# One ring of four PSUM banks for scans and dense stages, half stacks, and a new order of work in a two-layer attention kernel

## Chip, cores and metric

The kernel runs on one core of one Trainium2 chip. The metric is the device time of one execution in microseconds (us), the median of several runs; lower is better.

## What is computed

Two transformer blocks follow each other over `x` of 8 batches x 512 tokens x 256 features, all in float32. Both are modulated by a condition vector per batch. Each has 16 attention heads of 16 features. The first is causal and has a gelu MLP of width 1024; the second is not causal and has no MLP.

```python
# layer 0 (causal), cut
mod = silu(condition) @ Wada + bada          # shifts, scales, gates, one row a batch
xm = layernorm(x) * (1 + sc_a) + sh_a
q, k, v = split(xm @ Wqkv)                   # 16 heads of 16
attn = softmax(where(causal, q @ k.T * scale, -inf))
x = x + gt_a * ((attn @ v) @ Wproj + bproj)
xm = layernorm(x) * (1 + sc_m) + sh_m
x = x + gt_m * (gelu(xm @ W1 + b1) @ W2 + b2)
# layer 1, cut
h = gamma * layernorm(x) + beta
q, k, v = split(h @ Wqkv.T + bqkv)
h1 = (softmax(q @ k.T) / 16 @ v) @ Wp.T + bp + x
out = gamma * layernorm(h1) + beta + h1
```

## The kernel before

**Two passes over the scores.** The softmax needs each row's maximum, and the kernel gets it by computing the scores twice. A *scan* (token `s`) is one product of 128 query rows with the keys of one head, in bf16: `scan` on TensorE writes it into a PSUM bank `SX`, and VectorE reduces it to 128 maxima with one `reduce_max` (L738). Layer 0 scans are 128, 256, 384 and 512 columns wide, with a second small matmul for the causal mask (L936); layer 1 scans are 512 wide. A batch and layer has 64 scans, so the program has 1024. Later the same scores are computed again, transposed, in three banks `SC` (tokens `a` for three heads and `p` for the fourth), ScalarE takes their exponential into `E`, and the products with `V` (token `o`) accumulate in the bank `OP`, which ScalarE copies out (token `t`).

**Stacks.** To be exact enough in bf16, q and k are cut into three bf16 parts (`PART`), and 96 rows hold six products of parts. DMAs issued on SyncE (SP) bring the parts into these rows: six of 256 KB for a q stack (`stackq0`, `stackq1`) and six for a k stack (`stackk0`, `stackk1`). A scan waits on `stack_dma[layer]` for all twelve.

**Dense stages.** Everything else on TensorE goes through two banks `DN`: `turn_a`, `turn_m`, `turn_1` (transposes of the normed rows), `q0`, `k0`, `v0`, `q1`, `k1`, `v1`, `proj0`, `proj1`, `up_0` to `up_7`, `down_0` to `down_3`, and `max...` (transposes of the cut maxima, which POOL makes in `nm...`). ScalarE or VectorE reads each bank and adds to `dense_done`.

**Banks.** PSUM has eight: three `SC`, two `DN`, two `SX`, one `OP`. A dense stage waits for the dense reader two banks back, a scan for the scan reader two back. Neither ever waits for the other kind:

```python
wait(pe, dense_done, c.at(1, k - 1))          # bank(k), dense
return DN[(c.index() + k) % 2]
bank = SX[at["scan"].index() % 2]             # scan
wait(pe, scan_done, at["scan"].at(1, -1))
```

**Order.** All engines walk one list of tokens, written out by hand: `HEAD` (batches 0 and 1), `RING` once for each middle pass (five times), `TAIL` (the last ones). In a pass, layer 0 of batch i, layer 1 of batch i-1 and the first 41 scans of layer 0 of batch i+1 are woven together. Each engine executes its own instructions strictly in list order and waits on semaphores, so an instruction that waits holds back all that stands behind it on its engine. `pack`, `recip` and `scale` bring the softmax sums through DMAs to the projection: SP gathers sums and products (`RS`, `OC`), VectorE takes reciprocals (L873), SP writes and spreads them (`RB`), VectorE multiplies (L877). At the start, the modulation (`mods`, matmuls L888) stands between `q0` and `k0`, and `rows` (L978) behind.

Of the kernel before, what the change touches and what calls it, by code (L numbers as in the profile page):

```python
# [43 lines left out]
MASKED = -3.0e38  # L44

# [13 lines left out]
    stat_a norm_a turn_a q0 mods stackq0 k0 stackk0 rows s s s s s s s s s s s s s s s s s s nm0_0 s s max0_0 s  # L59
    s v0 s s s s s a row0 p s s s a s keep0 s p nm0_1 s s s s a s max0_1 s s s s p s s s s o s a s s s p a o s p  # L60
    a t nm0_2 s fold0_0 s s p a max0_2 p s o a p s s a s s p stat_a a o p s s s norm_a t a s fold0_1 p a s o s
    nm0_3 turn_a p max0_3 q0 a p o a p a t p o fold0_2 a p o t fold0_3 merge0 proj0 k0 stackq0 v0 norm_m turn_m
    stackk0 s s up_0 s s up_1 s s s s up_2 s s s s up_3 s s s s s s s s s up_4 s s up_5 s up_6 s s s s up_7 s s
    s s down_0 s s s s down_1 s s nm0a max0a down_2 s s down_3 s a s row0 s s norm_1 keep0 p a s s turn_1 s s s
    s q1 p s stackq1 stat_a o s k1 s stackk1 a v1 p a s s p a s s p o s s t a s s p s o s s s nm0b a s s p max0b
    s s s a s s s s s s p hold1 a p s o s a s s p s s s s s a s s s t p s s a s o s s s p a s s p o s nm1a s a s
    t s s p s s max1a s a s o p norm_a a s p a s p o s t s a p s pack0 s s recip0 a o turn_a p s s s q0 a scale0
    s v0 s p proj0 norm_m s a k0 o s t stackq0 p s a turn_m s s s up_0 s s up_1 stackk0 p s up_2 s up_3 s nm1b s
    s s a s up_4 s s up_5 s up_6 up_7 s p o s s max1b a s s down_0 s p s s a s s down_1 p s a o s s down_2 s s t
    p down_3 a o s s norm_1 p a s p s o t a s s s p s a s s nm0a p s o s a s p s turn_1 s s s max0a s a q1 p s  # L70
    k1""".split()
RING = """
    row0 o s s a stackq1 p s s a stackk1 t s p s s s s s s o s s a pack1 s s p s a row1 s p s s s a s s p s s nm0b
    s s recip1 o s s a s s p s s s max0b t s s s s a s scale1 p s a s o s s p a s o s p s a s p s t proj1 s a s p
    a o p a s p s s s o keep0 gain1 s t a s p s a o nm1a close1 s p s stat_a a max1a s v1 p s a o norm_a s t p s
    turn_a pack0 s a s s recip0 q0 s p s a o s stackq0 s p a scale0 s s p k0 a s s proj0 s s norm_m p v0 a o s p s
    t turn_m a s s o p s s a s up_0 s p stackk0 s up_1 s up_2 s s nm1b o s s up_3 s hold1 s up_4 s s max1b s s
    up_5 s s up_6 s s up_7 s s a s down_0 p s s a s down_1 s t p s down_2 s a s s p down_3 a o s p s a s p s s
    norm_1 o s s t a s s turn_1 s nm0a s s p s max0a a s o p s s a s q1 s p k1""".split()
TAIL = """  # L80
    s o row1 row0 a s t s s stackq1 stackk1 p s s a s p s s s s a s o s s s p s a p s s pack1 a s s o s p s s s
    nm0b a s s s p s t max0b s s a s o s s p s s a s p s recip1 a s s s o p s s a s s s s s p s a s t s s o p s
    s a s p s a s p s o nm1a s scale1 t a s s p max1a a o p s a p s proj1 a s p o gain1 s t v1 a s s pack0 p a s
# [37 lines left out]
for _n in ("norm_m", "norm_1", "norm_a"):  # L121
    ADDS[_n] = {"norm": 1}
ADDS["norm_m"]["bias"] = 1
COUNTS = ("dense", "res", "bias", "maxima", "max0", "max1", "hold", "pack", "sums", "scale", "rows0",
          "rows1", "x_in", "gain", "close", "stack0", "stack1", "high", "low", "norm", "head", "tick",
          "step", "masked", "group", "scan", "halves", "fold")


class Count:
# [999 lines left out]
```

## Time and profile before

| | |
|---|---|
| median of 3 runs | 1383.65 us (1379.31 to 1385.65) |
| the profiled execution | 1379.89 us, of which the span 1378.1 us |
| TensorE busy | 1242.5 us, 90% of the span |
| VectorE busy | 868.4 us, 63% |
| ScalarE busy | 672.3 us, 49% |
| GpSimd busy | 278.5 us, 20% |
| mean granted TensorE clock | 0.952 of 2.4 GHz |
| a middle pass | 151 to 154 us (the same product of the pass starts at 493.32, 647.43, 801.28 and 952.84 us) |

The span is the time from the first to the last instruction of the profiled execution. Busy time is the union of an engine's instructions. Matmuls overlap in the pipeline and their ends are modelled, so the busy time of TensorE also covers short waits between them; where two matmuls start is the surer measure. Names such as `SX<-KS,QS` say which tile is written from which; L933 is a line of the kernel.

### The profile page before, as it was taken

The numbers are of one execution on the slowest core, as the hardware profiler recorded it, in microseconds if no ns is written. First come the engines' busy times: TensorE is split into PE (matmuls) and PEld (weight loads), VectorE is DVE, ScalarE is ACT, GpSimd is POOL, SyncE is SP. The second block draws the span as 40 slices with busy tenths as digits, with TensorE's granted clock in tenths as the row PEclk, the third lists the DMA queues.
The fourth block names the chain that finished last, engine by engine and source line by source line (L and its number), as shares of the span: only waits on it lengthen the run. The fifth ranks groups of instructions, "written<-read, shape, count | busy, mean of one in ns | idle before, by whom it ended". The sixth has DMA issues, their size and how long they took to land.

```text
span 1378.1 us, 18596 instructions
## 1 busy us (share of the span) xinstructions
PE 1242.5 (90%) x6604; PEld 596.1 (43%) x6604; DVE 868.4 (63%) x1779; ACT 672.3 (49%) x1338; POOL 278.5 (20%) x378
## 2 busy tenths in 40 slices
PE   6687878999999998999899999999899998997786
PEld 4234443345344543446344543445344632453232
DVE  3553457654787467865787468865887477723664
ACT  1153224564555554655555565555456465555263
POOL 1123012120233012321132013311132012110002
PEclk9799988999999999999999999999999998999698
DMA  5603013130515024320515033510614050202101
GB/s 149 184 2 88 5 47 77 34 92 17 117 49 124 1 64 101 77 65 17 130 35 124 1 78 87 112 31 17 148 34 115 11 114 19 57 1 66 44 18 39
DMA packets 56118, 89.34 MB, mean 65 GB/s; under 512 B 9842, under 2 KB 20690, under 8 KB 56026
## 3 DMA queue, kind: packets, MB, share of 16 engines
q1 hardware_dynamic: 55006, 87.34, 26.4%
q8 instruction: 53, 0.87, 0.3%
q10 hardware_dynamic: 1020, 0.81, 0.2%
q14 instruction: 39, 0.32, 0.1%
HBM read 24.41 MB, written 4.70 MB: 21 GB/s over the span
## 4 chain that ended last, share of the span: by engine, by line
PE 69%; DVE 13%; ACT 6%; issue 2%; DMA 1%; POOL 1%; SPq 1%; ACTq 0%; DVEq 0%; POOLq 0%
PE DN L992 16%; PE OP L912 12%; PE SX L933 11%; PE SC L923 10%; DVE MX L738 9%; PE DN L1041 8%; PE DN L1017 7%; ACT E L599 4%; PE DN L1005 2%; PE SX L936 2%; DMA KS<-PART 1%; PE DN L1070 1%; DVE OUT L788 1%; SPq L476 1%; DVE PART L816 0%
## 5 line engine op out<-in xcount | busy, mean ns | idle before, releaser
L738 DVE TENSOR_REDUCE MX<-SX 128x1 f32<-128x512 f32 (+3 forms) x1024 | 556.4, 584 | 280.5 <-PE SX L936 174.0
L599 ACT ACTIVATE E<-SC 128x512 f32<-128x512 f32 (+3 forms) x1024 | 461.0, 523 | 383.6 <-PE SC L923 307.9
L933 PE MATMUL SX<-KS,QS 96*128 96x512 bf16 (+3 forms) x1024 | 342.7, 360 | 80.0 <-DVE MX L738 52.3
L923 PE MATMUL SC<-QS,KS 99*128 99x512 bf16 (+3 forms) x1024 | 280.8, 348 | 17.4 <-ACT E L599 10.1
L933 PEld LDWEIGHTS SX<-KS,QS 96*128 96x128 bf16 x1024 | 99.0, 98 | 294.7 <-DVE MX L738 172.9
L912 PE MATMUL OP<-E,V 128*32 128x512 f32 (+3 forms) x2048 | 216.5, 541 | 2.9 <-DVE X L808 1.4
L923 PEld LDWEIGHTS SC<-QS,KS 99*128 99x128 bf16 x1024 | 95.6, 99 | 164.8 <-ACT E L599 101.5
L517 POOL TENSOR_SCALAR_AFFINE_SELECT E<-E 128x512 f32<-128x512 f32 x128 | 85.7, 672 | 339.6 <-ACT E L599 339.6
L1041 PE MATMUL DN<-XT,W 128*128 128x512 f32 x256 | 123.7, 608 | 0.8 <-ACT HID L651 0.3
L1017 PE MATMUL DN<-XT,WQKV 128*128 128x512 f32 x256 | 121.8, 620 | 0.9 <-ACT XT L632 0.9
L992 PE MATMUL DN<-W,HID 128*128 128x256 f32 x512 | 117.1, 382 | 0.0
L936 PE MATMUL SX<-CAUSAL,ID 128*128 128x128 bf16 x512 | 112.6, 226 | 0.0
L912 PEld LDWEIGHTS OP<-E,V 128*32 128x32 f32 x2048 | 54.9, 112 | 110.1 <-issue 83.6
L992 PEld LDWEIGHTS DN<-W,HID 128*128 128x128 f32 x512 | 95.3, 190 | 14.1 <-ACT HID L651 0.3
L531 POOL TENSOR_TENSOR RSTD<-VE,HALF 128x4 f32<-128x4 f32 x32 | 32.9, 1029 | 296.1 <-DVE VE L750 295.3
L651 ACT ACTIVATE HID<-DN,VF 128x512 f32<-128x512 f32 x64 | 44.0, 687 | 66.7 <-PE DN L1041 66.2
L1017 PEld LDWEIGHTS DN<-XT,WQKV 128*128 128x128 f32 x256 | 49.1, 199 | 53.5 <-issue 49.1
L844 DVE TENSOR_TENSOR TMP<-DN,ROW 128x512 f32<-128x512 f32 x32 | 22.0, 689 | 78.2 <-PE DN L992 78.2
L552 POOL TENSOR_SCALAR NMP<-MX 128x32 bf16<-128x32 f32 (+1 forms) x36 | 8.6, 240 | 279.7 <-DVE MX L738 232.6
L992 PE MATMUL DN<-WP,OC 128*128 128x256 f32 x256 | 63.6, 406 | 1.4 <-ACT OC L657 1.4
L1041 PEld LDWEIGHTS DN<-XT,W 128*128 128x128 f32 x256 | 45.8, 192 | 42.7 <-issue 33.5
L936 PEld LDWEIGHTS SX<-CAUSAL,ID 128*128 128x128 bf16 x512 | 51.5, 101 | 25.6 <-issue 14.7
(92 smaller groups left out, 915.5 us busy)
## 6 DMA issues: line engine op xcount, KB each, us to landing
QS<-PART SPq DMA_DIRECT2D x96, 256.0 KB, 4.8
KS<-PART SPq DMA_DIRECT2D x96, 256.0 KB, 6.5
OC<-OE SPq DMA_DIRECT2D x56, 128.0 KB, 5.4
RB<-recip_sums SPq DMA_DIRECT2D x56, 128.0 KB, 2.6
XIN<-in_x SPq DMA_DIRECT2D x8, 512.0 KB, 4.2
ROW<-row_vectors SPq DMA_DIRECT2D x8, 512.0 KB, 3.6
out<-OUT SPq DMA_DIRECT2D x7, 512.0 KB, 3.2
W<-in_w SPq DMA_DIRECT2D x2, 1024.0 KB, 8.2
```

Source lines behind the costliest of these rows:

```text
L517: g.affine_select(out=block, in_=block, compare_op=ALU.is_ge, fill=zero, base=0, pattern=[[0, 4], [1, P]], channel_multiplier=-1)\
L531: g.tensor_tensor(RSTD[:], VE[:], HALF[:], ALU.pow).then_inc(rstd_pool, 1)
L599: a.activation(E[:, at["tick"].index() % 3, j, lo:T], SC[(at["head"].index() + j) % 3][:, lo:T], ACT.Exp, scale=HD ** -0.5 if layer == 0 e ...
L651: a.activation(HID[:, ht, :], bank(0)[:], ACT.Gelu, bias=B1[:, ht:ht + 1])\
L738: v.reduce_max(MX[:, qt, h:h + 1], SX[at["scan"].index() % 2][:, 0:w], AX.X, negate=True)\
L912: ins = t_.matmul(OP[32 * j:32 * j + 32, lo:T], V[layer][:, kt, h * VW:h * VW + 32], E[:, (at["step"].index() + n) % 3, j, lo:T], start=kt ...
L923: t_.matmul(SC[(at["head"].index() + j) % 3][:, lo:T], KS[layer][0:ALL_ROWS, h, kt * P:kt * P + P], QS[layer][0:ALL_ROWS, h, lo:T], start= ...
L933: ins = t_.matmul(bank[:, 0:w], QS[layer][0:CUT_ROWS, h, qt * P:qt * P + P], KS[layer][0:CUT_ROWS, h, 0:w], start=True, stop=layer == 1)
L936: ins = t_.matmul(bank[:, qt * P:w], ID16[:], CAUSAL[:], start=False, stop=True)
L992: ins = t_.matmul(psum[:, t % 2 * D:t % 2 * D + D], rows[:, kt, t * P:t * P + P], weights(kt), start=kt == 0, stop=kt == depth - 1)
L1017: ins = t_.matmul(psum[:], WQKV[n][:, kt, lo:lo + P], XT[:, kt, :], start=kt == 0, stop=kt == KT - 1)
L1041: ins = t_.matmul(psum[:], W1[:, kt, ht * P:ht * P + P], XT[:, kt, :], start=kt == 0, stop=kt == KT - 1)
```

## The change

Four things change. First, the banks `DN` and `SX` become one ring of four, `X`. Each scan takes one turn in it, and each dense stage one or two; a pair of `down` stages shares one. The new function `claim` lets TensorE wait for the last reader of the bank that it takes, whichever kind that reader was. Second, a stack is loaded in two halves of eight heads: twelve DMAs of 128 KB instead of six of 256 KB, with a semaphore for each half, so that scans of heads 0 to 7 wait for the first half only; the columns of the q and k weights are reordered on the host so that a half is 64 partitions. Third, at the start `k0` stands ahead of `mods`. Fourth, all three lists are new.

```diff
+BANKS = 4
...
-    stat_a norm_a turn_a q0 mods stackq0 k0 stackk0 rows s s s s s s s s s s s s s s s s s s nm0_0 s s max0_0 s
...
+    stat_a norm_a turn_a q0 stackq0 k0 mods stackk0 rows s s s s v0 s s s s s s s s s s s s s s s s s nm0_0 s s
...
+for _n, _adds in ADDS.items():
+    if "dense" in _adds and not _n.startswith("down"):
+        _adds["bank"] = _adds["dense"]
+ADDS["down_0"]["bank"] = ADDS["down_2"]["bank"] = 1
...
-        DN = [pb(f"DN{i}", [P, T]) for i in range(2)]
-        SX = [pb(f"SX{i}", [P, T]) for i in range(2)]
+        X = [pb(f"X{i}", [P, T]) for i in range(BANKS)]
...
-                    for part, ready in enumerate(marks[what[5:]]):
-                        wait(sp, (high_act, cut_low, cut_low)[part], ready)
-                        for r in range(CUTS):
-                            if parts[r] == part:
-                                sp.dma_start((QS, KS)[side][n][r:CUT_ROWS:CUTS, :, :], PART[:, side, part, :, :])\
-                                    .then_inc(stack_dma[n], 16)
+                    for half in range(2):
+                        rows = slice(P // 2 * half, P // 2 * half + P // 2)
+                        heads = slice(H // 2 * half, H // 2 * half + H // 2)
+                        for part, ready in enumerate(marks[what[5:]]):
+                            wait(sp, (high_act, cut_low, cut_low)[part], ready)
+                            for r in range(CUTS):
+                                if parts[r] == part:
+                                    sp.dma_start((QS, KS)[side][n][r:CUT_ROWS:CUTS, heads, :],
+                                                 PART[rows, side, part, :, :]).then_inc(stack_dma[n][half], 16)
...
+            def claim(n, done, value):
+
+                if n - BANKS in last_read:
+                    before, count = last_read.pop(n - BANKS)
+                    wait(pe, before, count)
+                last_read[n] = (done, value)
...
-                    wait(pe, stack_dma[layer], 192 * (b + 1))
-                bank = SX[at["scan"].index() % 2]
-                wait(pe, scan_done, at["scan"].at(1, -1))
+                    wait(pe, stack_dma[layer][h // (H // 2)], 192 * (b + 1))
+                claim(at["bank"].at(), scan_done, at["scan"].at(1, 1))
+                bank = X[at["bank"].index() % BANKS]
...
-                    wait(pe, dense_done, c.at(1, k - 1))
-                    return DN[(c.index() + k) % 2]
+                    if what in ("down_1", "down_3"):
+                        return X[marks["down"]]
+                    claim(at["bank"].at(1, k), dense_done, c.at(1, k + 1))
+                    marks["down"] = (at["bank"].index() + k) % BANKS
+                    return X[marks["down"]]
...
-        return w.reshape(-1, H // 2, 2, HD).transpose(0, 2, 3, 1).reshape(-1, D)
+        return w.reshape(-1, 2, H // 4, 2, HD).transpose(0, 3, 1, 4, 2).reshape(-1, D)
```

The first place is TensorE at the very start. L1017 (now L1044) is a projection of q or k, L888 (L903) the modulation, L978 (L1002) the gate rows, L933 (L957) a scan. Before:

```order
L1017 MATMUL DN0<-XT,WQKV0 128x512 x2
L1017 MATMUL DN1<-XT,WQKV0 128x512 x2
L888 MATMUL SC1<-CS,HID 128x8 x16
L888 MATMUL SC1<-CT,E 128x8 x8
L1017 MATMUL DN0<-XT,WQKV0 128x512 x2
L1017 MATMUL DN1<-XT,WQKV0 128x512 x2
```

and with the change:

```order
L1044 MATMUL X2<-XT,WQKV0 128x512 x2
L1044 MATMUL X3<-XT,WQKV0 128x512 x2
L1044 MATMUL X0<-XT,WQKV0 128x512 x2
L1044 MATMUL X1<-XT,WQKV0 128x512 x2
L903 MATMUL SC1<-CS,HID 128x8 x16
L903 MATMUL SC1<-CT,E 128x8 x8
```

The four matmuls of K now follow those of Q, and the modulation comes behind them.

The second place is TensorE in a middle pass, some 10 us behind `k1`, where scans of layer 0 stand densest. L912 (L927) is the product with V, L923 (L938) a score. Before, six scans stand in a row:

```order
L933 MATMUL SX0<-KS0,QS0 128x384
L936 MATMUL SX0<-CAUSAL,ID16 128x128
L933 MATMUL SX1<-KS0,QS0 128x512
L936 MATMUL SX1<-CAUSAL,ID16 128x128
L933 MATMUL SX0<-KS0,QS0 128x128
L936 MATMUL SX0<-CAUSAL,ID16 128x128
L933 MATMUL SX1<-KS0,QS0 128x256
L936 MATMUL SX1<-CAUSAL,ID16 128x128
L933 MATMUL SX0<-KS0,QS0 128x384
L936 MATMUL SX0<-CAUSAL,ID16 128x128
L933 MATMUL SX1<-KS0,QS0 128x512
L936 MATMUL SX1<-CAUSAL,ID16 128x128
```

and with the change, at the same place of the pass:

```order
L957 MATMUL X0<-KS0,QS0 128x512
L960 MATMUL X0<-CAUSAL,ID16 128x128
L957 MATMUL X1<-KS0,QS0 128x128
L960 MATMUL X1<-CAUSAL,ID16 128x128
L927 MATMUL OP<-E,V0 32x512 x4
L927 MATMUL OP<-E,V0 32x384 x4
L957 MATMUL X2<-KS0,QS0 128x256
L960 MATMUL X2<-CAUSAL,ID16 128x128
L957 MATMUL X3<-KS0,QS0 128x384
L960 MATMUL X3<-CAUSAL,ID16 128x128
L957 MATMUL X0<-KS0,QS0 128x512
L960 MATMUL X0<-CAUSAL,ID16 128x128
```

The product now stands among the scans instead of behind six of them, and the banks go round in fours. The longest run of scans in `RING` is four instead of six, and the count of scans that are third or later in their run is 14 instead of 9.

The third place is TensorE in `TAIL`, where layer 1 of the last batch begins. Before, the scans come right behind the last product of the batch ahead:

```order
L1017 MATMUL DN1<-XT,WQKV1 128x512 x2
L912 MATMUL OP<-E,V1 32x512 x8
L933 MATMUL SX0<-KS1,QS1 128x512
L933 MATMUL SX1<-KS1,QS1 128x512
L933 MATMUL SX0<-KS1,QS1 128x512
```

and with the change `v1` (L1019) comes first:

```order
L1044 MATMUL X3<-XT,WQKV1 128x512 x2
L927 MATMUL OP<-E,V1 32x512 x8
L1019 MATMUL X0<-WQKV1,XT 128x256 x4
L1019 MATMUL X1<-WQKV1,XT 128x256 x4
L957 MATMUL X2<-KS1,QS1 128x512
L957 MATMUL X3<-KS1,QS1 128x512
L957 MATMUL X0<-KS1,QS1 128x512
```

The matmuls of `v1` moved ahead of the first scan that needs the K stack.

## Rows read from the trace of the kernel before

**Rows 1.** The page: the chain that ended last, by engine.

```profile
PE 69%; DVE 13%; ACT 6%; issue 2%; DMA 1%; POOL 1%; SPq 1%; ACTq 0%; DVEq 0%; POOLq 0%
```

**Rows 2.** Waits of TensorE, whole span: us in total, times, longest us.

```profile
PE SX L933 <- DVE MX L738: 52.3, 174, 2.9
PE SX L933 <- DMA KS<-PART: 22.2, 3, 11.8
```

**Rows 3.** Stretches of a middle pass: PE, PEld, DVE, ACT, POOL busy, clock, DMA.

```profile
665.00:675.00 10.00, 8.68 (x59) 2.79 (x62) 8.53 (x16) 4.88 (x10) 1.28 (x2) 1.00 1.06 228
675.00:685.00 10.00, 8.86 (x69) 3.57 (x61) 8.45 (x18) 4.75 (x14) 2.80 (x7) 1.00 0.60 143
685.00:695.00 10.00, 8.91 (x39) 2.85 (x39) 8.92 (x14) 4.12 (x13) 2.29 (x2) 0.71 0.38 111
...
705.00:715.00 10.00, 8.59 (x67) 2.90 (x70) 9.62 (x24) 6.58 (x18) 6.36 (x9) 1.00 0.00 0
715.00:725.00 10.00, 9.86 (x74) 6.16 (x67) 9.49 (x28) 5.21 (x13) 2.71 (x5) 1.00 0.18 58
```

**Rows 4.** Timeline of that pass, VectorE and TensorE: start us, us, what.

```profile
683.59 0.54 DVE L873 RECIPROCAL RR<-RS 128x64 f32<-128x64 f32 x1
684.07 6.89 DVE L738 TENSOR_REDUCE MX<-SX 128x1 f32<-128x512 f32 x11
...
743.76 3.62 PE L992 MATMUL DN<-WQKV,XT 128*128 128x256 f32 x16
```

**Rows 5.** Timeline of the start, TensorE, VectorE and SP.

```profile
16.62 5.40 PE L1017 MATMUL DN<-XT,WQKV 128*128 128x512 f32 x8 [0.92 <-ACT XT L632]
...
22.68 3.88 SPq L476 DMA_DIRECT2D QS<-PART  x6
...
24.14 1.23 DVE L816 TENSOR_TENSOR PART<-X,PART 128x1024 bf16<-128x1024 f32 x1
...
27.33 5.17 PE L1017 MATMUL DN<-XT,WQKV 128*128 128x512 f32 x8
...
42.63 0.29 PE L933 MATMUL SX<-KS,QS 96*128 96x128 bf16 x1 [8.82 <-DMA KS<-PART]
```

**Rows 6.** Timeline of VectorE in the first scans.

```profile
45.90 0.98 DVE L738 TENSOR_REDUCE MX<-SX 128x1 f32<-128x256 f32 x2 [0.40 <-PE SX L936]
47.13 0.89 DVE L738 TENSOR_REDUCE MX<-SX 128x1 f32<-128x512 f32 x2 [0.25 <-PE SX L936]
48.42 0.98 DVE L738 TENSOR_REDUCE MX<-SX 128x1 f32<-128x256 f32 x2 [0.40 <-PE SX L936]
```

**Rows 7.** DMA issues of the page: KB each, median us to landing.

```profile
OC<-OE SPq DMA_DIRECT2D x56, 128.0 KB, 5.4
RB<-recip_sums SPq DMA_DIRECT2D x56, 128.0 KB, 2.6
```

**Rows 8.** Timeline of TensorE where batch 1's K stack is awaited.

```profile
139.36 0.23 PE L933 MATMUL SX<-KS,QS 96*128 96x128 bf16 x1 [1.65 <-DMA KS<-PART]
```

**Rows 9.** Waits of TensorE for scan reductions, window 140:330 us.

```profile
PE SX L933 <- DVE MX L738: 12.7, 33, 2.9
```

**Rows 10.** Waits of TensorE for scan reductions, window 1104:1240 us.

```profile
PE SX L933 <- DVE MX L738: 6.1, 19, 0.9
```

**Rows 11.** Timeline of the last batch's layer 1, TensorE and SP.

```profile
1266.05 1.92 PE L912 MATMUL OP<-E,V 128*32 128x512 f32 x16
1279.72 1.03 PE L933 MATMUL SX<-KS,QS 96*128 96x512 bf16 x2 [11.75 <-DMA KS<-PART]
...
1282.58 1.21 PE L933 MATMUL SX<-KS,QS 96*128 96x512 bf16 x2 [0.19 <-DVE MX L738]
```

**Rows 12.** SP in the same stretch.

```profile
1263.73 4.07 SPq L476 DMA_DIRECT2D QS<-PART  x6
1267.85 4.25 SPq L476 DMA_DIRECT2D KS<-PART  x6
```

**Rows 13.** SP behind `stackk1` in the middle pass.

```profile
671.98 0.59 SPq L414 DMA_DIRECT2D RS<-OE  x1
```

More of the change, by code:

```diff
@@ L64 @@
[L64 to L68, printed above, removed]
@@ new lines @@
+    turn_1 s a s s stat_a s q1 s p a s k1 stackq1 p s s o v1 s t a s s p s s s s s stackk1 s a s s nm0b p s
+    max0b s a o s p s a s o norm_a s s p s a p s t s s a s o p s s a p s a s s p s s s o s a t s s p turn_a s o
+    s a s p s a s p s s nm1a s o s t q0 max1a s pack0 recip0 v0 stackq0 s s s a s hold1 s s p s a p s o scale0 s
+    a proj0 p k0 a s p s norm_m s a s s o s s p turn_m stackk0 t s a s up_0 up_1 s p up_2 s s up_3 s up_4 up_5 s
+    s s s a s s up_6 s nm1b up_7 s s s p s o s s a s max1b p s down_0 down_1 s s a s o s p s down_2 s s a s p
@@ L234, in one_list @@
             at["scan"].n += 1
+            at["bank"].n += 1
         else:
@@ L356, in two_layers @@
         max_dma = [sem("max_dma0"), sem("max_dma1")]
-        stack_dma = [sem("stack_dma0"), sem("stack_dma1")]
+        stack_dma = [[sem(f"stack_dma{n}{half}") for half in "ab"] for n in range(2)]
         sums_dma = sem("sums_dma")
@@ L624, in bank @@
                     wait(act, dense_full, c.at(1, k + 1))
-                    return DN[(c.index() + k) % 2]
+                    return X[(at["bank"].index() + k) % BANKS]
                 if what in ("turn_a", "turn_m", "turn_1"):
@@ L637, in work @@
                     side = "qk".index(what[0])
-                    wait(act, stack_dma[0], at["stack0"].at(192))
-                    wait(act, stack_dma[1], at["stack1"].at(192))
+                    for half in range(2):
+                        wait(act, stack_dma[0][half], at["stack0"].at(192))
+                        wait(act, stack_dma[1][half], at["stack1"].at(192))
                     for t in range(2):
@@ L765, in bank @@
                     wait(dve, dense_full, c.at(1, k + 1))
-                    return DN[(c.index() + k) % 2]
-                if what == "mods" and b == 0:
+                    if what in ("down_1", "down_3"):
+                        return X[marks["down"]]
+                    return X[(at["bank"].index() + k) % BANKS]
+                if what in ("down_0", "down_2"):
+                    marks["down"] = at["bank"].index() % BANKS
+                elif what == "mods" and b == 0:
                     modulation()
```

57 lines of the change are left out of this document (30 added, 27 removed).

## The prediction

> **What bounds the kernel now.** I read the chain that ended last first. TensorE holds 69% of it and VectorE 13% [rows 1], so TensorE's own work sets most of the time, and what can be won is where it stands still. Next I read the waits of TensorE over the whole span. One wait leads, scan matmuls waiting for the reduction of an earlier scan, 52.3 us in 174 waits; three waits for K stacks add 22.2 us [rows 2]. Both are what the change is about, so 74.5 us is visible to it. More is hidden, because a short wait between two pipelined matmuls still reads as busy.
>
> The next question is whether a deeper ring can win these waits back or whether VectorE is itself full there. For this I read one middle pass in stretches of 10 us. In 665 to 695 and 705 to 725 TensorE has its holes, and VectorE is busy 8.53, 8.45, 8.92, 9.62 and 9.49 us of 10 [rows 3]. So in the 50 us where scans stand densest VectorE works for 45.0 us and idles 5.0. The timeline agrees: eleven reductions of 512 columns run for 6.89 us without a hole, 0.63 us each, while TensorE waits for them [rows 4]. More banks do nothing for such a burst except to let TensorE run two scans further ahead. This is the main reason why I don't forecast all of the 52.3 us.
>
> **The start.** Today Q's matmuls end at 16.62 + 5.40 = 22.0 us, the modulation follows, K's start at 27.33, and the first scan starts at 42.63 after 8.82 us of waiting for the K stack [rows 5]. With K directly behind Q, its matmuls run from 22.0 to about 26, or to 27.2 at the 5.17 us that they took. From Q's last matmul to the end of its last cut VectorE needed 24.14 + 1.23 - 22.0 = 3.4 us [rows 5]; K needs the same, so its parts are ready at 29.4 to 30.6. SP then is the limit: the Q stack has twelve issues now. An issue takes 3.88/6 = 0.65 us at 256 KB [rows 5]. For 128 KB I take the same 0.65, since `OC` and `RB` of 128 KB are issued at nearly that pace. Twelve from 22.68 end at 30.4, the six of K's first half at 34.3, and the last lands 2.6 us after its issue by the 128 KB rows of `RB` [rows 7]: first scan at about 36.3 instead of 42.6. TensorE is free by then: the modulation, which filled 22.0 to 27.3, ends near 32. Gain **6.3 us**; bounds 3 (the landing takes 5.4 as for `OC`, [rows 7]) and 9 (half an issue's price for half the bytes).
>
> **The first scans.** From the start only scans run, and TensorE and VectorE wait for each other through two banks: four tiles take 48.42 - 45.90 = 2.52 us, of which VectorE reduces 0.98 + 0.89 = 1.87 [rows 6]. With four banks VectorE should run through: 0.47 us a tile instead of 0.63, over the 27 tiles that stand ahead of the first score **4.3 us**; bounds 0 and 4.3. Seventeen further scans move into this time, ahead of the first score.
>
> **Batch 1's K stack.** Two scans stood ahead of `up_0` and waited 1.65 us [rows 8]; now `up_0` and `up_1` come first. **1.7 us**, bounds 0 and 1.7.
>
> **140 to 330 us.** TensorE shows 12.7 us of waits for reductions, the longest 2.9 [rows 9]. Some are of the short kind that four banks remove, some are bursts; I take half, **6 us**, bounds 0 and 12.7.
>
> **The five middle passes.** The 5.0 us of VectorE idle above are one part of what can be won. The other is borrowing: TensorE may enter a dense stage or a product with two more scans queued for VectorE, 2 x 0.63 us in each of the two stretches, 2.5 us. Together 7.5 us is the upper bound, nothing the lower. I take **4.4 us** a pass, somewhat over half, because products hold no bank and dense stages hold two of the four: ahead of products the queue really doubles, ahead of dense stages it doesn't. Also the densest burst of six is broken up while the lists as a whole put no fewer scans third in a run. Five passes: **22 us**, bounds 0 and 37.
>
> **The end.** The last batch's layer 1 has nothing else to do while its stacks load: TensorE stands from about 1268 to 1279.72 [rows 11]. `v1` fills 3.5 us of it (a `v` stage takes 3.62 us, [rows 4]). The K half: SP issues twelve DMAs from 1263.73 to 1272.10 today [rows 12], 3 MB that land by 1279.7. The change issues eighteen up to the end of K's first half, to about 1263.7 + 18 x 0.65 = 1275.4, and the last lands 2 to 2.6 us later: 1277.6, only **2.1 us** sooner, since Q's second half now goes ahead of K's first. Together **5.6 us**, bounds 3 and 7. The Trainium skill (DMA: Bandwidth & Descriptors, Rules for kernel authors) advises against splitting a transfer over partition halves, since both halves use the same DMA engines one after the other. The stacks here bear that out in bytes (3 MB in about 16 us either way), and by that rule alone the 2.1 us would be nothing, but a reader that needs only one half can gain from it. Behind it, pairs of scans of layer 1 take 1.21 + 0.19 = 1.40 us at half clock [rows 11], 0.70 a tile against 0.63 for VectorE alone [rows 4]: 18 tiles, **1.3 us**. The last passes, 1104 to 1240 us, show 6.1 us of waits [rows 10]; half is **3 us**.
>
> **What is added.** `claim` itself is a semaphore wait in place of another. SP issues 24 more DMAs a pass, 15.6 us; where that could be felt is the second rival. I cost them at nothing.
>
> **Sum.** 6.3 + 4.3 + 1.7 + 6 + 22 + 5.6 + 1.3 + 3 = 50.2 us. The profiled execution took 1379.9, so 1329.7; it lies 3.8 us under the median of the runs, which makes **1333**. All terms at their lower bounds leave 6 us of gain (1378), all at the upper ones 80 (1304).
>
> **Rivals.**
> *The middle passes don't move (1364).* If VectorE is the limit of the dense stretches [rows 3, 4], TensorE arrives earlier and waits longer, and only start, first scans, batch 1's stack and end are won: 6.3 + 4.3 + 1.7 + 5.6 + 1.3 = 19.2 us, 1383.7 - 19.2 = 1364. For it: 96% in 705 to 715. Against it: 85% in the two stretches before. 17%.
> *SP late for the sums (1343).* `pack1` stands behind `stackk1` on SP, and VectorE stands still at the reciprocal until `RS` has landed, with every scan behind it. Today `RS` is issued at 671.98 [rows 13] and the reciprocal runs at 683.59 without a wait [rows 4]: 11.6 us, less 5.4 to land [rows 7] leaves 6.2. Twelve more issues are 7.8 us. So 1.6 us are missing in each of six passes, about 10 us. Against it: in the new list Q is projected earlier before K, and SP can start sooner. It shrinks the gain and doesn't turn it. 10%, mostly inside my range.
> *Slower (1405).* Dense stages and scans now wait for each other. A pass has 36 dense claims, the program 288. In a ring of four a dense stage behind a burst finds a bank whose reduction is still queued on VectorE, and then waits up to one reduction, 0.63 us; all matmuls, scores too, stand behind it. At 0.25 us each it costs 72 us against 50 gained: 1405. It decides from 0.18 us a claim. For it: VectorE is up to 96% busy [rows 3], and today no such wait can exist. Against it: at such a place the next scan would have met the same backlog, so most of it takes the place of a wait that is there today. 8%.
> *The clock (1348).* 685 to 695 has a granted clock of 0.71 [rows 3]: TensorE fell from 2.4 to 1.2 GHz after 20 us with holes, for 5.8 us, which costs at most half of that, 2.9. If holes come in another rhythm and one such stretch more falls in each of five passes, 15 us are lost: 1348. The Trainium skill (TensorE: Matmul & The Clock Gate, A second HAM failure mode) tells of a kernel that went round PSUM banks and lost clock by small idle times between groups; the ring has that form, but here holes exist before and shrink. 5%.
> *The change wins no time (within 0.5%, 1377 to 1390)*: 6%. *More than I count, under 1315*, since hidden waits are won too: 8%.
>
> **Numbers.** The forecast case, 1315 to 1350, has 46% alone and takes in the SP case; with the clock and deeper cases around it the range 1304 to 1365 leaves out about 2 in 10. Its low end is all upper bounds, its high end the case in which the middle passes don't move. A measurement of this kernel tells 0.5% (7 us) from no change. Faster by more than that: 86%; within it: 6%; slower: 8%.
>
> **What would show it.** First scan near 36 us; reductions of the first scans back to back; a middle pass some 4 us shorter; waits of scans for reductions well under 52.3 us in total, with VectorE above 90% in the dense stretches; the gap before the last layer 1's scans near 6 us. I am wrong if the reciprocal (L873's successor) waits for `RS`, if dense lines show waits for reductions of scans, or if the passes keep their length.

## The result and the profile after

The changed kernel takes **1286.9 us** (median of 4, 1285.2 to 1290.0) against 1381.5 for the kernel before on the same chip: the ratio is **0.932** [0.929, 0.935]. That is faster, as forecast, but by 94.6 us where 50 were forecast, and below the low end of the range (1304). The profiled execution took 1288.15 us, its span is 1286.4.

The page of the changed kernel: the engines' busy time, the granted clock in 40 slices (tenths), the chain that ended last by engine, and the issues of the stacks.

```profile
PE 1198.2 (93%) x6604; PEld 593.7 (46%) x6604; DVE 858.4 (67%) x1779; ACT 688.6 (54%) x1356; POOL 273.5 (21%) x378
...
PEclk9789999999999999999999999999999999999698
...
PE 69%; ACT 9%; SPq 8%; DVE 7%; issue 3%; DMA 3%; POOL 1%; ACTq 0%; DVEq 0%; POOLq 0%
...
QS<-PART SPq DMA_DIRECT2D x192, 128.0 KB, 2.3
KS<-PART SPq DMA_DIRECT2D x192, 128.0 KB, 2.4
```

VectorE fell from 13% to 7% of the chain [rows 1]; ScalarE and SP's issues took over part of it. The mean granted clock of the span rose from 0.952 to 0.969.

TensorE's waits in the changed kernel over the whole span (us in total, times, longest us). L957 is the scan (L933 before), L938 a score, L1019, L1032, L1068 and L1097 are dense stages.

```profile
PE SC L938 <- ACT E L607: 12.0, 39, 1.2
PE X L957 <- DMA KS<-PART: 8.9, 3, 5.5
PE X L957 <- DVE MX L747: 8.9, 35, 0.8
PE X L1032 <- DVE XN L797: 5.9, 2, 4.5
...
PE X L957 <- ACT HID L660: 1.9, 7, 0.7
```

The 52.3 us of [rows 2] are 8.9, and the 22.2 us for K stacks are 8.9 too. These two rows account for 56.7 of the 91.7 us between the two spans. The rest has no row of its own: it lies in waits too short to show as one, and in the clock. To see it I added up, for every matmul, the time from its start to the start of the next, less what its columns take at 2.4 GHz. Of this excess the lower clock gets its share of the time by the granted clock at that time, and the rest is standing still, put down to what the next matmul was.

| us, whole span | before | changed | ring_only | order_only | order_ring | scan_two | scan_three |
|---|---|---|---|---|---|---|---|
| still ahead of scans | 137.5 | 47.9 | 84.3 | 204.0 | 58.0 | 218.6 | 99.0 |
| still ahead of scores | 54.2 | 63.0 | 65.6 | 53.1 | 63.9 | 50.6 | 56.6 |
| still ahead of dense stages | 39.3 | 46.2 | 53.6 | 40.4 | 46.5 | 33.6 | 40.0 |
| all standing still | 243.4 | 173.8 | 217.5 | 299.1 | 182.6 | 299.4 | 205.6 |
| lower clock | 55.8 | 34.6 | 52.1 | 103.3 | 29.2 | 117.5 | 44.8 |

(The last five are kernels of the experiments below. "All" holds products with V and masks too.) From the first matmul to the last, what is left when both are taken off is 1063 to 1070 us in every kernel. From before to changed, standing still falls by 69.6 us and the clock's cost by 21.2, 90.8 together, nearly the 91.7 between the spans. Ahead of scans alone TensorE won 89.6 us, and 20 came back elsewhere, 15.7 of them ahead of scores and dense stages. The split between the last two rows is a choice, since time that TensorE stands still at the lower clock could go to either. If the clock is charged only with the second time that columns take at 1.2 GHz, its cost is 46 us before and 28 changed, and standing still falls by 74 us: the two parts are good to some 4 us.

By stages, counted from the start of each `up_0`, against the terms of the prediction:

| stretch | before, us | changed, us | won | forecast |
|---|---|---|---|---|
| start to first `up_0` | 139.7 | 125.9 | 13.8 | 12.3 |
| to the second `up_0` | 150.9 | 131.3 | 19.6 | 6 |
| next five passes, each | 157.9, 154.1, 153.9, 151.5, 151.7 | 151.5, 145.4, 147.4, 144.6, 145.8 | 6.4, 8.7, 6.5, 6.9, 5.9 | 4.4 |
| to the last `up_0` | 150.3 | 143.8 | 6.5 | 3 |
| from it to the end | 168.1 | 150.7 | 17.4 | 6.9 |

The last two lines of the table belong together. The new `TAIL` takes 21 matmuls, some 6 us of TensorE's own work, ahead of the last `up_0` instead of behind it (587 matmuls behind it before, 566 changed), so 6 of the 17.4 us were moved and not won there. Together the two stretches won 23.9 us where the terms make 9.9. The last stretch before and then changed, in the columns explained below:

```profile
1209.99:1378.14 168.15, 134.90 (x587) 57.18 (x587) 78.43 (x149) 74.48 (x132) 18.50 (x28) 0.88 0.14 34
```

```profile
1135.68:1286.40 150.72, 126.97 (x566) 54.44 (x566) 74.31 (x144) 68.98 (x126) 16.54 (x27) 0.90 0.14 38
```

The windows of two other stretches show both effects. Columns: window, us; busy time and count of PE, PEld, DVE, ACT, POOL; granted clock; DMA share; GB/s. In the kernel before:

```profile
139.70:290.60 150.90, 132.98 (x645) 64.03 (x643) 95.82 (x192) 57.50 (x119) 29.12 (x38) 0.90 0.23 52
602.60:756.50 153.90, 147.79 (x810) 71.45 (x810) 106.84 (x219) 83.26 (x168) 34.83 (x44) 0.98 0.29 69
```

and in the changed kernel:

```profile
125.90:257.20 131.30, 121.53 (x641) 61.69 (x641) 91.66 (x185) 54.90 (x116) 29.52 (x38) 0.96 0.23 67
554.10:701.50 147.40, 143.48 (x810) 71.62 (x810) 104.76 (x219) 87.48 (x171) 34.22 (x45) 0.99 0.26 72
```

Busy TensorE time itself fell, by 11.5 us in the first stretch with nearly the same matmuls (641 for 645): a matmul at 1.2 GHz reads as a longer busy one. In the middle pass the 810 matmuls are the same, and VectorE's 219 instructions too, yet the pass is 6.5 us shorter. VectorE was busy 106.8 of 153.9 us there, so over the whole pass it wasn't full, only over the dense stretch.

The start and the end, where single steps can be read. The changed kernel's SP and TensorE at the start (start us, us, engine, line, what):

```profile
22.76 8.28 SPq L484 DMA_DIRECT2D QS<-PART  x12
31.09 7.65 SPq L484 DMA_DIRECT2D KS<-PART  x12
...
36.64 0.29 PE L957 MATMUL X<-KS,QS 96*128 96x128 bf16 x1 [1.35 <-DMA KS<-PART]
...
45.41 0.39 PE L957 MATMUL X<-KS,QS 96*128 96x512 bf16 x1 [0.20 <-DVE MX L747]
...
47.00 0.39 PE L957 MATMUL X<-KS,QS 96*128 96x512 bf16 x1 [0.20 <-DVE MX L747]
```

The first scan starts at 36.64 (forecast 36.3, before 42.63 [rows 5]). Four tiles take 47.00 - 45.41 = 1.59 us, against 2.52 before [rows 6], and VectorE reduces 22 tiles in a row without a hole:

```profile
43.67 8.57 DVE L747 TENSOR_REDUCE MX<-X 128x1 f32<-128x128 f32 x22
```

And its end, TensorE and SP:

```profile
1189.26 1.92 PE L927 MATMUL OP<-E,V 128*32 128x512 f32 x16
1191.11 3.72 PE L1019 MATMUL X<-WQKV,XT 128*128 128x256 f32 x16
1200.29 10.44 PE L957 MATMUL X<-KS,QS 96*128 96x512 bf16 x19 [5.46 <-DMA KS<-PART]
```

The gap ahead of the last layer 1's scans is 5.46 us where it was 11.75 [rows 11]; near 6 was forecast. In SP's queue the time from `QS`'s first issue to the first scan is 1200.29 - 1186.95 = 13.3 us, where it was 1279.72 - 1263.73 = 16.0 [rows 11, 12].

```profile
1186.95 7.70 SPq L484 DMA_DIRECT2D QS<-PART  x12
1194.69 7.66 SPq L484 DMA_DIRECT2D KS<-PART  x12
```

### The profile page after: what moved, and what is told of

The parts are those of the page before. It is cut to its first block, busy times and chain, and to the rows that moved or that the text cites. A ratio compares the mean times of both kernels' runs of the same rounds, so it can differ in the third digit from the quotient of the medians.

```text
span 1286.4 us, 18823 instructions
## 1 busy us (share of the span) xinstructions
PE 1198.2 (93%) x6604; PEld 593.7 (46%) x6604; DVE 858.4 (67%) x1779; ACT 688.6 (54%) x1356; POOL 273.5 (21%) x378
## 4 chain that ended last, share of the span: by engine, by line
PE 69%; ACT 9%; SPq 8%; DVE 7%; issue 3%; DMA 3%; POOL 1%; ACTq 0%; DVEq 0%; POOLq 0%
PE X L1019 17%; PE OP L927 12%; PE SC L938 10%; PE X L957 10%; PE X L1068 8%; PE X L1044 8%; ACT E L607 7%; SPq L484 6%; DVE MX L747 3%; PE X L1032 2%; DMA OC<-OE 2%; PE X L960 1%; SPq L421 1%; PE X L1097 1%; DVE XN L797 1%
## 5 line engine op out<-in xcount | busy, mean ns | idle before, releaser
L747 DVE TENSOR_REDUCE MX<-X 128x1 f32<-128x512 f32 (+3 forms) x1024 | 535.9, 585 | 182.2 <-PE X L960 111.7
L957 PE MATMUL X<-KS,QS 96*128 96x512 bf16 (+3 forms) x1024 | 309.4, 353 | 22.6 <-DMA KS<-PART 8.9
L938 PE MATMUL SC<-QS,KS 99*128 99x512 bf16 (+3 forms) x1024 | 284.0, 347 | 21.7 <-ACT E L607 12.0
L927 PE MATMUL OP<-E,V 128*32 128x512 f32 (+3 forms) x2048 | 212.9, 533 | 4.2 <-ACT OE L622 3.1
L938 PEld LDWEIGHTS SC<-QS,KS 99*128 99x128 bf16 x1024 | 95.4, 98 | 192.0 <-ACT E L607 116.8
L957 PEld LDWEIGHTS X<-KS,QS 96*128 96x128 bf16 x1024 | 98.6, 99 | 175.3 <-DVE MX L747 59.8
L1068 PE MATMUL X<-XT,W 128*128 128x512 f32 x256 | 121.9, 607 | 3.3 <-ACT XT L640 2.7
L1044 PE MATMUL X<-XT,WQKV 128*128 128x512 f32 x256 | 118.2, 605 | 1.0 <-ACT XT L640 1.0
L1019 PE MATMUL X<-W,HID 128*128 128x256 f32 x512 | 115.6, 381 | 0.5 <-ACT HID L660 0.5
L960 PE MATMUL X<-CAUSAL,ID 128*128 128x128 bf16 x512 | 106.3, 223 | 0.0
L927 PEld LDWEIGHTS OP<-E,V 128*32 128x32 f32 x2048 | 54.5, 111 | 107.7 <-issue 73.8
L1019 PEld LDWEIGHTS X<-W,HID 128*128 128x128 f32 x512 | 96.0, 190 | 15.3 <-issue 1.1
L1044 PEld LDWEIGHTS X<-XT,WQKV 128*128 128x128 f32 x256 | 47.5, 194 | 52.3 <-issue 47.7
L1068 PEld LDWEIGHTS X<-XT,W 128*128 128x128 f32 x256 | 46.3, 192 | 47.6 <-issue 44.6
L1019 PE MATMUL X<-WP,OC 128*128 128x256 f32 x256 | 60.4, 389 | 2.4 <-issue 0.8
L960 PEld LDWEIGHTS X<-CAUSAL,ID 128*128 128x128 bf16 x512 | 51.3, 100 | 23.9 <-issue 11.0
```

The source lines that it names most:

```text
L747: v.reduce_max(MX[:, qt, h:h + 1], X[at["bank"].index() % BANKS][:, 0:w], AX.X, negate=True)\
L927: ins = t_.matmul(OP[32 * j:32 * j + 32, lo:T], V[layer][:, kt, h * VW:h * VW + 32], E[:, (at["step"].index() + n) % 3, j, lo:T], start=kt ...
L938: t_.matmul(SC[(at["head"].index() + j) % 3][:, lo:T], KS[layer][0:ALL_ROWS, h, kt * P:kt * P + P], QS[layer][0:ALL_ROWS, h, lo:T], start= ...
L957: ins = t_.matmul(bank[:, 0:w], QS[layer][0:CUT_ROWS, h, qt * P:qt * P + P], KS[layer][0:CUT_ROWS, h, 0:w], start=True, stop=layer == 1)
L960: ins = t_.matmul(bank[:, qt * P:w], ID16[:], CAUSAL[:], start=False, stop=True)
L1019: ins = t_.matmul(psum[:, t % 2 * D:t % 2 * D + D], rows[:, kt, t * P:t * P + P], weights(kt), start=kt == 0, stop=kt == depth - 1)
```

## The experiments

The experiments ran at three later times, on three chips, where the kernel before took 1381.4 us (the parts apart), 1381.5 (depth and half reductions) and 1383.8 (the single steps). The ratios are to the kernel before on the same chip at the same time. Where kernels of different times are compared and differ by 2 to 6 us, the medians alone don't settle it.

Two theories stood first for the 44 us that the forecast missed. **A, depth**: four banks let TensorE run ahead, and that wins more than I allowed. **B, order**: the new lists space scans better, and win on their own. Later came **D**, the new lists live on scans that run three or four deep, and its rival **E**, what the new lists need of the ring is banks for the dense stages.

### The parts apart

**ring_only**: the kernel before with the ring of four and its claims; old lists and whole stacks. A pair of `down` stages keeps its bank of the ring while the scans between them go round, so three scans of `HEAD` that stood between `down_0` and `down_1` stand ahead of `down_0`.

```diff
-        DN = [pb(f"DN{i}", [P, T]) for i in range(2)]
-        SX = [pb(f"SX{i}", [P, T]) for i in range(2)]
+        X = [pb(f"X{i}", [P, T]) for i in range(BANKS)]
...
-                wait(pe, scan_done, at["scan"].at(1, -1))
+                claim(at["bank"].at(), scan_done, at["scan"].at(1, 1))
```

> The lists and the whole stacks of before, with the ring of four banks (three scans of batches 0 and 1 are moved from behind down_0 to ahead of it, since a pair of down stages holds a bank). Theory A (depth: short waits for a scan bank, visible and hidden, are what is won, and any order wins them): 1325 to 1345, waits of scans for reductions under 20 us. Theory B (order: the lists move VectorE's load out of the dense stretches, the ring alone only lets TensorE arrive earlier at the same VectorE): 1360 to 1378, waits of scans still over 35 us.

Measured: 1350.4 us, 0.975 [0.972, 0.978]; 31 us won. That lies between the two forecasts; the waits (12.9 us, below) are those of theory A.

**order_only**: the changed kernel with its new lists, but two banks for scans, two for dense stages and whole stacks.

```diff
-        X = [pb(f"X{i}", [P, T]) for i in range(BANKS)]
+        DN = [pb(f"DN{i}", [P, T]) for i in range(2)]
+        SX = [pb(f"SX{i}", [P, T]) for i in range(2)]
...
-                claim(at["bank"].at(), scan_done, at["scan"].at(1, 1))
+                wait(pe, scan_done, at["scan"].at(1, -1))
```

> The new lists (K behind Q with them) with two dense and two scan banks and whole stacks. Theory A (depth): only start and end are won, 1355 to 1375, and scans wait for reductions 45 us or more. Theory B (order): most is won, 1305 to 1330.

Measured: 1489.1 us, 1.075 [1.071, 1.080]; **108 us slower** than before, which neither theory had.

**order_ring**: the changed kernel with whole stacks, so new lists and ring.

```diff
-                    wait(pe, stack_dma[layer][h // (H // 2)], 192 * (b + 1))
+                    wait(pe, stack_dma[layer], 192 * (b + 1))
```

> New lists and ring, whole stacks. If half stacks are worth what the start and the end show (first scan and last layer-1 scan some 2 to 4 us sooner each): 1290 to 1296. If the twelve shorter issues also matter in the middle passes through the sums behind them on SP, it would be faster than the change: under 1285.

Measured: 1292.9 us, 0.935 [0.931, 0.938].

**order_half**: new lists and half stacks, with two and two banks as in order_only.

> New lists and half stacks, two dense and two scan banks. Against the full change this takes the ring alone away. Theory A (depth): 1345 to 1370. Theory B (order): 1297 to 1320.

Measured: 1477.0 us, 1.067 [1.064, 1.070], again far outside both.

The first three and the kernel before make a square:

| us | old lists | new lists |
|---|---|---|
| two and two banks | 1381 | 1489 |
| ring of four | 1350 | 1293 |

The ring is worth 31 us under the old lists and 196 under the new ones; the new lists cost 108 us without the ring and win 57 with it. Both theories fall: the gain is in neither part, and a sum over the parts, which my prediction was, can't give it. Half stacks win 12 us without the ring (1489.1 to 1477.0, same chip and time) and perhaps 6 in it (1292.9 to 1286.9, at two times and with intervals that overlap).

TensorE's waits show the same. In order_only:

```profile
PE SX L933 <- DVE MX L738: 122.8, 261, 3.0
PE SC L923 <- ACT E L599: 12.5, 40, 1.2
PE SX L933 <- DMA KS<-PART: 12.5, 3, 8.6
```

and in ring_only:

```profile
PE X L953 <- DMA KS<-PART: 22.8, 4, 11.8
PE X L953 <- DVE MX L743: 12.9, 57, 0.5
PE SC L934 <- ACT E L604: 12.6, 45, 0.6
PE X L953 <- ACT HID L656: 11.6, 18, 1.5
```

The last row there is new. Under the old lists the ring ends the waits for reductions (52.3 to 12.9, none over 0.5 us), and 11.6 us return as scans that wait for ScalarE to read an `up` stage's bank: the shared ring's own wait, the reverse of the one that my slower rival named. The new lists have 1.9 of it. By the count in the result's table the ring wins 53.2 us ahead of scans under the old lists, and 25.7 of them return ahead of scores and dense stages: TensorE runs ahead with its scans and then stands at the next thing. Under the new lists the ring wins 146.0 ahead of scans, and 16.9 return (order_only against order_ring). A middle pass (the same columns as above), first of ring_only, then of order_only:

```profile
583.80:736.70 152.90, 145.73 (x810) 71.86 (x809) 106.75 (x219) 82.77 (x167) 33.74 (x44) 0.98 0.30 69
```

```profile
638.40:809.00 170.60, 153.34 (x810) 72.41 (x810) 107.77 (x219) 88.19 (x171) 34.11 (x44) 0.95 0.28 62
```

With the old lists the ring wins 1 us in this pass (152.9 for 153.9), with both 6.5 are won, and new lists alone lose 17. Over all five middle passes, from the second `up_0` to the seventh, the ring alone wins 0.2 us in all, both together 34.4 (6.9 a pass), and the new lists alone lose 77.7 (15.5 a pass). What the ring wins under the old lists lies wholly outside the middle passes: 6.1 us up to the first `up_0`, 10.0 up to the second, 7.3 up to the last and 5.9 behind it.

What do the new lists ask for? On TensorE, where tokens of other engines don't break a run of scans, 17 scans of a middle pass stand third or later in their run instead of 12 (not the 14 and 9 given with the change). Here is how long TensorE stood still ahead of scans in the same pass, by their place in the run. The clock is charged as in the second split above and the floor is the columns alone, so the sums are somewhat above those of the first table's count.

| us, one middle pass | before | ring_only | order_only | changed |
|---|---|---|---|---|
| first in its run | 5.3 | 4.7 | 6.5 | 2.2 |
| second | 3.3 | 2.9 | 10.6 | 1.1 |
| third or later | 4.1 | 1.5 | 7.6 | 1.5 |

Of the 12 us that order_only loses here 7.3 stand ahead of the second scan of a run and 3.5 ahead of the third or later. So it is not mainly longer runs that ask for depth; the runs follow each other more closely, and a second scan meets the reductions of the run before it. In the whole program 572 scans have less than 1.1 us of TensorE's columns between their start and that of the scan two before them, where it was 473, and two reductions take 2 x 0.58 us on average.

### How deep

Both kernels are the changed one with one more wait of each scan: for the reduction of the scan two before it (**scan_two**), or three before it (**scan_three**). The ring, its order and the banks of the dense stages stay.

```diff
                 claim(at["bank"].at(), scan_done, at["scan"].at(1, 1))
+                wait(pe, scan_done, at["scan"].at(1, -1))
```

with `at(1, -2)` in scan_three.

> The full change, but a scan also waits until the scan before last has been reduced, so that no more than two scans are outstanding as before; dense stages keep the ring. Theory D (the new lists live on scans queued three and four deep): within 15 us of the 1477 of the new lists with two and two banks. Theory E (dense stages are what needed the third and fourth bank): under 1320.

Measured: 1500.1 us, 1.084 [1.080, 1.089].

> The same with three scans outstanding. Theory D: between, 1310 to 1380, if both further places count; near 1290 if the third alone is enough. Theory E: 1287.

Measured: 1330.9 us, 0.963 [0.960, 0.967].

So 1500, 1331 and 1287 us for scans two, three and four deep. Scan_two keeps every bank of the dense stages and is as slow as order_only: E falls. D holds in kind, though scan_two lies 23 us above the 1477 where 15 were allowed. A third scan under way is worth 169 us and a fourth 44. The same scan wait in scan_two and scan_three, TensorE over the whole span:

```profile
PE X L958 <- DVE MX L747: 144.3, 285, 3.1
```

```profile
PE X L958 <- DVE MX L747: 43.4, 113, 2.4
```

Against the changed kernel's 8.9, the waits that show grew by 135 and 34.5 us, and the times by 213 and 44. The rest is in the table: shorter stops ahead of scans, and the clock, whose cost rose from 34.6 us to 117.5 in scan_two (granted 0.917) and 44.8 in scan_three (0.964).

### Is VectorE the bound

My forecast held back because VectorE looked full where scans stand densest. These two kernels shorten its largest job: the reduction reads only the first half of each scan's columns. The maxima leave the other columns out; all else is as before (**before_half_reduce**) or as changed (**after_half_reduce**).

```diff
-                v.reduce_max(MX[:, qt, h:h + 1], SX[at["scan"].index() % 2][:, 0:w], AX.X, negate=True)\
+                v.reduce_max(MX[:, qt, h:h + 1], SX[at["scan"].index() % 2][:, 0:w // 2], AX.X, negate=True)\
```

> The kernel before with each scan's reduction over the first half of its columns only (the maxima leave out the other half). If VectorE's work is the bound of the dense stretches, as the prediction took it from 85 to 96% busy: the middle passes become 12 us or more shorter, 1290 or less in all. If the round trip through two banks is: reductions are 0.13 to 0.27 us shorter but the trip stays, 1330 to 1360.

Measured: 1321.4 us, 0.957 [0.953, 0.960].

> The changed kernel with the same half reductions (again half the columns are left out of the maxima). If VectorE's work still bounds stretches of it: 1260 or less. If the ring has made it all but free of VectorE: 1270 to 1287.

Measured: 1265.5 us, 0.916 [0.913, 0.919].

Cheaper reductions win 60 us before and 21 after the change. VectorE's busy time falls alike, from 858.4 us to 655.0 in the changed kernel. Both times lie between the two forecasts that were made for them (1290 and 1330, 1260 and 1270). The stages say more. Before, the shorter reductions win 5.0 us in each middle pass, where 12 or more were forecast if VectorE's work were the bound. In the changed kernel they win 1.3 there, and 16.0 of the 24.8 us between the spans lie ahead of the second `up_0` and behind the last. So in the changed kernel's middle passes VectorE's work hardly bounds TensorE. A shorter reduction also frees its bank sooner, so before_half_reduce alone can't tell VectorE's throughput from the time until a bank comes free. But deeper scans with the right order win more with full reductions (94.6 us) than half reductions do with two banks (60), so most of what reductions cost TensorE before was the time until a bank came free.

### The single steps at start and end

**mods_first**: the changed kernel with the modulation ahead of `k0`, where it stood before.

```diff
-    stat_a norm_a turn_a q0 stackq0 k0 mods stackk0 rows s s s s v0 s s s s s s s s s s s s s s s s s nm0_0 s s
+    stat_a norm_a turn_a q0 mods stackq0 k0 stackk0 rows s s s s v0 s s s s s s s s s s s s s s s s s nm0_0 s s
```

> The changed kernel with the modulation ahead of stackq0 and k0 again, as before. The prediction's start term stands if the first scan comes near 42 us instead of 36.6 and the whole is 5 to 7 us slower than the change: 1292 to 1294. If later scans make up for the late start: 1287 to 1289.

Measured: 1290.3 us, 0.933 [0.931, 0.936]. Its first scan comes late by 7.0 us:

```profile
43.63 0.29 PE L957 MATMUL X<-KS,QS 96*128 96x128 bf16 x1 [4.84 <-DMA KS<-PART]
```

but its first `up_0` only by 4.0 (129.95 for 125.94), so of the 7 us at the first scan 3 are caught up before it. The median is 3.4 us higher, at another time; against the kernel before the two are 0.933 and 0.932, which the measurement can't tell apart.

**v1_late**: the changed kernel with `v1` of the last batch behind 21 of the scans that now follow it (two scans behind `max1_0`).

```diff
-    a p a o p a p turn_1 o a t p q1 a o p a p k1 stackq1 stackk1 o v1 s s s s s s s s s s s s s s s s s s nm1_0
-    s max1_0 t s s s s s s s a s pack1 s p s s a s s s nm1_1 p s a s p s s max1_1 a s s o p s s a s s p s s s a
+    a p a o p a p turn_1 o a t p q1 a o p a p k1 stackq1 stackk1 o s s s s s s s s s s s s s s s s s s nm1_0
+    s max1_0 t s s v1 s s s s a s pack1 s p s s a s s s nm1_1 p s a s p s s max1_1 a s s o p s s a s s p s s s a
```

> The changed kernel with the last batch's v1 behind the first scans again. The term of the end stands if the gap before the last layer-1 scans grows by 3.5 us, to about 9, and the whole is 3 to 4 us slower: 1290 to 1291. If v1 in its late place is hidden behind VectorE's reductions: 1286 to 1288.

Measured: 1291.0 us, 0.933 [0.929, 0.936]. The gap is 3.7 us wider, which is `v1`:

```profile
1204.74 10.44 PE L957 MATMUL X<-KS,QS 96*128 96x512 bf16 x19 [9.13 <-DMA KS<-PART]
```

and from the last `up_0` to the end it takes 154.5 us instead of 150.7. The medians differ by 4.2 us, but at two times, and the ratios (0.933 and 0.932) don't tell them apart; the trace is the better witness here.

**first_halves**: a better version. The prediction noted that Q's second half goes ahead of K's first, though the first scans don't read it. At the two places where TensorE stands waiting for a stack, SP now issues Q's first half, K's first, Q's second, K's second.

```diff
+                    if (n, b) not in ((0, 0), (1, B - 1)):
+                        load(side, 0)
+                        load(side, 1)
+                    elif side == 0:
+                        load(0, 0)
+                    else:
+                        load(1, 0)
+                        load(0, 1)
+                        load(1, 1)
```

> The changed kernel with SP's issues in another order at two places only, batch 0's layer 0 and batch 7's layer 1: Q's first half, K's first half, then both second halves. K's first half is then complete six issues (3.9 us) sooner. If the gaps there are set by SP's issues: the gap at the end falls from 5.5 to about 1.6 us, the first scan comes 1 us sooner, 1281 to 1284. If the DMA engines' bytes set them, or second halves then come late: 1286 or more.

Measured: 1282.3 us (median of 5, 1278.9 to 1286.1), 0.928 [0.925, 0.930]: 4.6 us under the changed kernel, at another time and with intervals that overlap. SP at the start and TensorE at the end:

```profile
23.01 3.86 SPq L484 DMA_DIRECT2D QS<-PART  x6
26.92 3.82 SPq L484 DMA_DIRECT2D KS<-PART  x6
30.78 4.60 SPq L484 DMA_DIRECT2D QS<-PART  x6
35.43 3.79 SPq L484 DMA_DIRECT2D KS<-PART  x6
...
1191.53 1.04 PE L967 MATMUL X<-KS,QS 96*128 96x512 bf16 x4 [1.60 <-DMA KS<-PART]
```

At the end the gap of 5.46 us is 1.60, and the last stretch 146.4 us for 150.7; at the start the first scan comes 1.65 us sooner (34.99) and the first `up_0` 2.8. By its median it is the fastest kernel here that leaves nothing out; what the traces show of it is the two gaps.

## Why the prediction was right or wrong

The direction was right and the size wrong. The spans differ by 91.7 us and the sum had 50.2. Of the missing 41.5 us, 13.6 lie between the first and the second `up_0`, 12.4 in the five middle passes, 14.0 behind them and 1.5 ahead of the first `up_0`. By kind, standing still fell by 69.6 us where the sum had 50.2, and the lower clock's cost by 21.2 where it had nothing. Two steps failed above all: the new lists were put at next to nothing beside the ring, and half of the waits that the rows show was taken for what four banks can win, with the whole of them as the upper bound.

**The start (6.3 us): the step held, its worth was smaller.** Twelve issues took 8.28 us (7.7 forecast), K's first half six at the forecast pace, and the first scan came 0.3 us after the forecast. The first scan came 6.0 us sooner than before. By mods_first the moved `mods` alone is 7.0 us at the first scan but 4.0 at the first `up_0`; what of it reaches the end of the kernel its median doesn't resolve. In the whole first stretch 13.8 us were won against 12.3 in three terms.

**The first scans (4.3 us): right in kind, a little low.** 1.59 us for four tiles is 0.40 a tile (0.47 forecast, 0.63 before), and VectorE runs through. At that pace 27 tiles would win 6.2 us (an estimate).

**Batch 1's K stack (1.7 us): right, and paid back.** The wait of 1.65 us ahead of `up_0` is gone, but a new one for a K stack stands 75 us further on:

```profile
200.32 0.60 PE L957 MATMUL X<-KS,QS 96*128 96x512 bf16 x2 [2.13 <-DMA KS<-PART]
```

**140 to 330 us (6 us): mis-sized.** The step that failed is "some are of the short kind that four banks remove, some are bursts; I take half". From the first to the second `up_0` 19.6 us went. TensorE's waits for reductions in just this stretch, before and then changed:

```profile
PE SX L933 <- DVE MX L738: 12.0, 32, 2.9
```

```profile
PE X L957 <- DVE MX L747: 2.3, 7, 0.7
```

So 9.7 us of visible waits went where I took 6, nearly all and not half. And the granted clock rose from 0.90 to 0.96: by the count of the result's table its cost in this stretch fell from 14.7 us to 5.3. That half of the 19.6 had no term in my sum, and with it the stretch passed the term's upper bound of 12.7.

**The five middle passes (22 us at 4.4 each): the step that failed.** It was said to be "somewhat over half" of a bound of 7.5; they won 5.9 to 8.7 us each, 6.9 on average, so the bound itself nearly held. The size was off by half, the reason by more: standing still ahead of scans fell from 10.8 to 3.3 us in the pass of the windows above, of which the row of waits had shown 4.1.

```profile
PE SX L933 <- DVE MX L738: 4.1, 16, 0.8
```

"TensorE may enter a dense stage or a product with two more scans queued" was costed for the ring, and the lists were given next to nothing ("the lists as a whole put no fewer scans third in a run"). The runs show otherwise: over the five middle passes the ring alone wins 0.2 us, the lists alone lose 77.7, and it takes both to win 34.4. The count of scans third in a run, by which I judged the lists, was the wrong one: most of what they lose without depth stands ahead of the second scan of a run. Why the same lists win with depth (the scores and products that they put between scans, or where they set the dense stages) no run takes apart.

**VectorE as the bound ("the main reason why I don't forecast all of the 52.3 us"): wrong as a limit.** The 50 us that I read had 5.0 us of VectorE idle, and I took that for the pass. A pass is 154 us, VectorE busy for 107 of them, so there was room outside the dense stretches. before_half_reduce still won 60 us, so reductions did set part of the time, but mostly by how long they held a bank.

**The end (5.6, 1.3 and 3 us): the gap right, the rest too small.** `v1` filled what it should (3.7 us by v1_late, 3.5 forecast), and K's half brings the first scan 2.7 us nearer to SP's first issue (2.1 forecast). Yet the last two stretches won 23.9 us, where my terms make 9.9 and their upper bounds 14.4. Behind the last `up_0` 17.4 us went, 6 of them work that the new list takes earlier. By the count, standing still ahead of scans fell there from 24.0 us to 8.4. The gap explains 6.3 of these 15.6; the other 9.3 are short stops, which the two terms for pace (1.3 and 3) undersized. order_ring has 16.4 of the 17.4 us already (151.7 for 168.1), so they belong to ring and lists, not to the halves. ring_only, which moves no work, has 5.9 of them.

**The clock.** The only step that named it was a loss. It was a gain of 21.2 us by the count above (17 by the second split): TensorE was at the lower level for about 2 x (1 - 0.952) x 1378 = 132 us before and 80 after. With the lists alone it fell to 0.925. In the main, where TensorE stood still less it was granted more: 299 us of standing still go with 0.917 and 0.925, 174 and 183 with 0.969 and 0.972. The runs show the two side by side; which hole costs which stretch stays open, and part of it is not the program's: on one chip the kernel before ran from 1377.1 us at a clock of 0.955 to 1385.6 at 0.947. The Trainium skill (TensorE: Matmul & The Clock Gate, A second HAM failure mode) tells of a kernel that went round PSUM banks, idled briefly between its groups of matmuls, and moved back and forth between the two clock levels. Here the ring of four goes with the higher clock (0.956 for 0.952 with the old lists, 0.972 for 0.925 with the new), so going round the banks doesn't by itself lose it.

**The rivals.** *The middle passes don't move*: true of the old lists in the ring, not of the change. *SP late for the sums*: the reciprocal now waits for `RS`, 3.9 us in all in seven waits, not 10:

```profile
DVE RR L888 <- DMA RS<-OE: 3.9, 7, 0.9
```

*Slower, by dense claims behind scan reductions*: 2.4 us in five waits, where 72 would have been needed.

```profile
PE X L1097 <- DVE MX L747: 1.8, 3, 1.3
...
PE X L1019 <- DVE MX L747: 0.3, 1, 0.3
...
PE X L1068 <- DVE MX L747: 0.3, 1, 0.3
```

*More than I count* came true, at 8%. The reason written beside it, hidden waits, is about half of what the sum missed, the clock the other half. I had seen the first: "more is hidden, because a short wait between two pipelined matmuls still reads as busy". I didn't count them. Standing still ahead of scans was 137.5 us in all, of which the row of waits for reductions showed 52.3. Where the upper bounds of my sum came from such rows (12.7 us for 140 to 330, 6.1 for the last passes) they were passed, and the range's low end lay 17 us above the result.

## What to carry to other kernels

When a change adds buffers and reorders the work, the two can't be costed apart: ask of the new order how many buffers it needs, and of the buffers which order can use them; here the order alone was 108 us slower, the ring alone 31 faster, and both together 88 faster. Bound a gain of depth by start-to-start times of the engine that waits, not by its rows of waits, and give the clock a term of its own in the direction in which the holes move. When a transfer is split so that a reader can start early, order the queue by what the reader needs first.

## What was unexpected in the hardware

- An issue of SP costs nearly the same for half the bytes: 0.64 to 0.69 us at 128 KB (7.66/12 and 8.28/12), 0.65 to 0.71 at 256 KB [rows 5, 12]. Twice the DMAs are nearly twice the queue's time.
- A half stack's DMA lands 2.3 to 2.4 us after its issue (the page's rows above), though `OC` of the same 128 KB took 5.4 [rows 7]; in the changed kernel `OC` itself takes 3.8:

```profile
OC<-OE SPq DMA_DIRECT2D x56, 128.0 KB, 3.8
```

- The kernels' mean granted clock ran from 0.917 (scan_two) to 0.982 (after_half_reduce), in nearly the reverse order of their times, with the same number of matmuls on TensorE, 6604, in each.
